# A new order of steps in the first two token blocks, score banks turned round, and a wait taken out of the last expert

## The chip, the cores and the metric

The kernel is one program on one NeuronCore of a Trainium2 chip. The metric is the device time of one execution in microseconds (us), lower is better. The engines are named as in the profile: PE is TensorE (PEld its weight loads), DVE is VectorE, ACT is ScalarE, POOL is GpSimd, SP is SyncE, which here only issues DMAs.

## What is computed

An input x of 4 x 1024 tokens with 256 features goes through gated cross-attention and a gated mixture of experts:

```python
x = x + tanh(g_xattn) * attention(layernorm(x), ctx, ctx)   # 16 heads of 16, 77 context rows per batch
h = layernorm(x)                                            # with gain and bias
logits = h @ Wr                                             # 7 experts, top 2 chosen, softmax gates
routed = experts(h)       # capacity 732 tokens: silu(h @ W1[e]) * (h @ W3[e]) @ W2[e], times the gate
shared = silu(h @ W1s) * (h @ W3s) @ W2s                    # every token
x = x + tanh(g_ffn) * (routed + shared)
```

All is fp32. Each large product is made of three passes with operands split in a high and a low part (hi*hi, hi*lo, lo*hi), so most tiles exist twice: a cast gives the high part, a subtraction the low one.

## The kernel before, in words

**Blocks.** The 4096 tokens are 8 blocks of 512 (four tiles of 128). Attention of block b and the shared network of block b-1 are interleaved by hand in one list of steps for each period: `first_period` (block 0), `second_period` (block 1), `period` (blocks 2 to 6, in a loop of two and one more) and `last_period` (block 7). Each engine walks through the same list and takes out of it the steps that it has code for, so the list sets every engine's own order, and each engine runs strictly in that order, stopping at semaphores. After the blocks come the seven experts (`expert`), each with weights that have been loaded and split while the one before ran.

**Attention of a block.** PE transposes normalized x (`transpose_x`), makes the queries (`queries`), and computes per tile of 128 tokens scores against all keys only for their maxima (`maxima`; DVE reduces them, and the next tile's matmuls use the same banks and wait for that reduction). `maxima_T` transposes the 16 x 512 maxima, ACT copies them out (`mtr`), SP stacks them by DMA under the queries in `qst` (`stack_maxima`), where keys `kst` carry a row of -1 for each head, so that one matmul of 112 rows gives scores less their maximum (`pair_scores`, a pair of heads p from 0 to 7). Pairs 0 and 1 are scored in `first_scores`, the others in `scores`, each pair in two of the four banks 0 to 3, followed by an exponential of 77 x 1024 on ACT (`exps`) and the products with the values (`pv`, two pairs at a time). DVE transposes the result back and divides; ACT and POOL split it (`attention_hi`, `attention_lo`), and PE projects it (`project`). DVE adds it to x and takes statistics, POOL makes the reciprocal root, DVE normalizes (`norm2`), PE transposes again (`transpose_z`), ACT and DVE apply gain and bias and split.

**Shared network.** `up(f)` is 12 matmuls of 512 columns in two banks (`up_a`, `up_b`), ACT's silu, DVE's product, a cast and a subtraction; `down(f)` is 12 matmuls of 256 columns over four tiles. Banks 0 to 2 rotate for `up`.

**Shared weights in the first block.** Six half matrices h = 0 to 5 (W1s, W3s, W2s) are loaded into staging areas that are used again (h = 4 uses the area of h = 2). ACT casts each in two pieces (`shared_hi`), POOL subtracts (`shared_lo`, one piece of 512 columns each, pieces 2h and 2h+1). SP loads h = 3 in the step `more_shared` after `xT_ready`, and h = 4 and 5 only after POOL's piece 5:

```python
if h > 3:
    sp.wait_ge(sig["wsplit_lo"], NSTEP0 + 6)
```

POOL's code for the step `scores` is `attention_lo`; in block 0 it waits there until all attention of the block is done. `keep_busy(j, n, ...)` is n small matmuls into bank j that compute nothing needed.

**Last expert.** Experts add their rows to the output with indirect DMAs that accumulate (L1084). The last expert's second half of rows is instead gathered from the output first (L1068, `rows_of_last`), added on DVE (L1652) and written back without accumulation.

Of the kernel before, what the change touches and what calls it, by code (L numbers as in the profile page):

```python
# [86 lines left out]
def first_period(do, b):  # L87
# [45 lines left out]
    do("scores", b, 1)  # L133
    do("queries", n)
# [12 lines left out]
    do("maxima", n, 2)  # L147


def second_period(do, b):  # L150
# [55 lines left out]
    up(6)  # L206
    nxt("maxima", 2)
    down(4)
    nxt("maxima", 3)
    do("pick", b, 1)  # L210
    down(5)
# [3 lines left out]
    nxt("exp_table")  # L215
    down(6)
    do("last_hidden", f)
    nxt("first_scores")
# [6 lines left out]
def period(do, b):  # L225
# [71 lines left out]
    down(5)  # L297
    nxt("maxima_T")
    nxt("stack_maxima")
    up(7)  # L300
    nxt("exp_table")
    if not odd:
        do("place", f, 0)
    down(6)
    do("last_hidden", f)
    nxt("first_scores")
# [166 lines left out]

def queries_bank(b):

    return 6 if b.at(1) else 4
# [33 lines left out]
def xT_bank(b):  # L510

    return 4 if b.at(1) else 6
# [31 lines left out]
def build(nc, a, out):  # L544
# [37 lines left out]
    mtr = ar(138, N)[0:H]  # L582

# [107 lines left out]
    qst0_loaded qst0_rest_loaded qst_loaded qst_rest_loaded kst_loaded kbd_spread heads_ready kbd_loaded vst_ready m_ready m_done mT_ready mtr_ready  # L691
# [35 lines left out]
    def q_of(b):  # L727

        return hTs[0] if b.at(0) else qT

# [8 lines left out]
    def _(sp):  # L739
# [29 lines left out]
        def first_keys():  # L769

            sp.wait_ge(sig["k_lo"], KD)
            for j in range(2):
                sp.dma_start(kscr[j].rearrange("(k p) t -> p k t", p=P), k_s[:, j].bitcast(F32)).then_inc(sig["k_stored"], 16)
# [5 lines left out]
        def load_keys(b):  # L779

            if b.c == 0:
# [9 lines left out]
                sp.wait_ge(sig["k_stored"], 32)  # L791
# [27 lines left out]
        def stack_rest(b):  # L819

            for r in (2, 3):
                for base in (0, 64):
                    sp.dma_start(qst[base:base + 32, r::4, :].bitcast(F32), q_of(b)[32 * r:32 * r + 32, 0].bitcast(F32)).then_inc(sig["qst0_rest_loaded"], 16)

        def stack_maxima(b):
            sp.wait_ge(sig["mtr_ready"], b.n + 1)

            first, rest = ("qst0_loaded", "qst0_rest_loaded") if b.at(0) else ("qst_loaded", "qst_rest_loaded")
            for r0, r1, loaded in ((0, 2, sig[first]), (2, NPAIR, sig[rest])):
                sp.dma_start(qst[96:112, r0:r1, :].bitcast(F32),  # L830
                             mtr[:, :].bitcast(F32).unsqueeze(1).broadcast_to([H, r1 - r0, N])).then_inc(loaded, 16)
                if b.at(0) and r0 == 0:
                    stack_first_lo((2, 3), sig[rest])
# [42 lines left out]
    def _(pool):  # L876
# [33 lines left out]
        def rest_const():  # L910
# [3 lines left out]
                                  pattern=[[1, P]], channel_multiplier=-1))  # L914
            do(pool.memset(vst[0:SK], 1.0))
# [147 lines left out]
        def rows_of_last(e):  # L1063
# [7 lines left out]
            pool.wait_ge(sig["rows_gathered"], 16 * (NR // 2))  # L1071
# [23 lines left out]
    def _(act):  # L1095
# [35 lines left out]
        def stack_hi(b):  # L1131
# [3 lines left out]
            for r in range(2):  # L1135
                for base in (0, 64):
                    act.dma_start(qst[base:base + 32, r::4, :].bitcast(F32), q_of(b)[32 * r:32 * r + 32, 0].bitcast(F32)).then_inc(sig["qst0_loaded"], 16)
# [5 lines left out]
        def transpose_x(b):  # L1143
            for k in range(KD):
# [9 lines left out]
        def maxima_T(b):  # L1154
            act.wait_ge(sig["mT_ready"], b.n + 1)
            if b.at(1):
                act.wait_ge(sig["qst0_loaded"], 112)
# [3 lines left out]
        def exps(b, p):  # L1161
# [5 lines left out]
            act.activation(prob[p % 4][0:SK], banks[0:SK, 2 * (p % 2):2 * (p % 2) + 2], ACT.Exp, scale=DH ** -0.5)\  # L1167
               .then_inc(sig["exp_done"], 1)

        def first_scores(b):  # L1170
            for p in range(2):
                exps(b, p)
# [970 lines left out]
```

## Time and profile before

| | us |
|---|---|
| median of three executions | 852.79 |
| lowest, highest | 852.49, 857.55 |
| profiled execution | 850.94 |
| its span (first to last instruction) | 849.2 |
| its mean granted TensorE clock, share of full speed | 0.997 |

The span is what the views below divide; 1.74 us of the profiled execution lie around it. Time stamps are from the start of the span. In a timeline row the numbers are start and duration (of one instruction, or from the first to the last of a merged run), then engine, line, operation, tile and count, and in brackets the idle time of that engine just before and what ended it.

### The profile page before, as it was taken

The numbers are of one execution on the slowest core, as the hardware profiler recorded it, in microseconds if no ns is written. First come the engines' busy times: TensorE is split into PE (matmuls) and PEld (weight loads), VectorE is DVE, ScalarE is ACT, GpSimd is POOL, SyncE is SP. The second block draws the span as 40 slices with busy tenths as digits, with TensorE's granted clock in tenths as the row PEclk, the third lists the DMA queues.
The fourth block names the chain that finished last, engine by engine and source line by source line (L and its number), as shares of the span: only waits on it lengthen the run. The fifth ranks groups of instructions, "written<-read, shape, count | busy, mean of one in ns | idle before, by whom it ended". The sixth has DMA issues, their size and how long they took to land.

```text
span 849.2 us, 14564 instructions
## 1 busy us (share of the span) xinstructions
PE 821.0 (97%) x5228; PEld 719.8 (85%) x5228; DVE 588.6 (69%) x1260; ACT 386.2 (45%) x660; POOL 321.6 (38%) x250
## 2 busy tenths in 40 slices
PE   8888999999999999999999999999999999999995
PEld 7474868868868688687788899999999999999995
DVE  7577788787788777888877666565656756566442
ACT  4547263373453633734445454453544545354331
POOL 7453103150032230303126405818275481834336
PEclk9999999999999999999999999999999999999998
DMA  8541411324104223130032624334444324431112
GB/s 265 136 125 28 125 38 35 90 53 119 19 25 124 43 52 85 34 100 14 26 125 53 194 75 108 71 83 105 110 88 88 102 46 112 98 76 17 16 25 38
DMA packets 92257, 67.24 MB, mean 79 GB/s; under 512 B 53556, under 2 KB 78984, under 8 KB 92200
## 3 DMA queue, kind: packets, MB, share of 16 engines
q1 hardware_dynamic: 39608, 54.79, 23.1%
q0 software_dynamic: 51744, 10.67, 8.8%
q10 hardware_dynamic: 848, 1.05, 0.5%
q8 instruction: 31, 0.51, 0.3%
q14 instruction: 26, 0.21, 0.1%
HBM read 37.75 MB, written 14.27 MB: 61 GB/s over the span
## 4 chain that ended last, share of the span: by engine, by line
PE 81%; DVE 4%; issue 3%; ACT 1%; POOL 1%; DVEq 0%; POOLq 0%; ACTq 0%
PE bank L1692 20%; PE bank L1694 20%; PE bank L1693 20%; PE bank L1993 3%; PE bank L1994 3%; PE bank L1995 3%; PE bank L1832 2%; PE bank L1826 2%; PE bank L1793 2%; PE bank L2035 1%; PE bank L1931 1%; PE bank L2019 1%; PE bank L1699 1%; PE bank L1922 1%; PE bank L1700 1%
## 5 line engine op out<-in xcount | busy, mean ns | idle before, releaser
L1692 PE MATMUL bank<-split_operands 128*128 128x366 f32 (+4 forms) x1104 | 364.9, 331 | 1.6 <-POOL split_operands L972 0.9
L1694 PE MATMUL bank<-split_operands 128*128 128x366 f32 (+4 forms) x1104 | 359.6, 326 | 0.0
L1693 PE MATMUL bank<-split_operands 128*128 128x366 f32 (+4 forms) x1104 | 359.5, 326 | 0.0
L1692 PEld LDWEIGHTS bank<-split_operands 128*128 128x128 f32 (+1 forms) x1104 | 205.8, 186 | 17.7 <-issue 5.9
L1694 PEld LDWEIGHTS bank<-split_operands 128*128 128x128 f32 (+1 forms) x1104 | 205.5, 186 | 10.6
L1693 PEld LDWEIGHTS bank<-split_operands 128*128 128x128 f32 (+1 forms) x1104 | 206.0, 187 | 8.1
L1084 POOL DMA_INDIRECT out<-float_data,scatter_now x42 | 120.1, 2860 | 170.1 <-DVE float_data L1655 146.7
L1675 DVE TENSOR_TENSOR hidden<-bank,float_data 128x366 f32<-128x366 f32 x112 | 60.5, 540 | 108.3 <-PE bank L1694 108.0
L1270 ACT ACTIVATE float_data<-bank 128x366 f32<-128x366 f32 x112 | 53.5, 477 | 110.2 <-PE bank L1694 110.2
L1267 ACT CAST split_operands<-hidden 128x366 fp32r<-128x366 f32 x112 | 55.7, 497 | 68.5 <-DVE hidden L1675 68.5
L1046 POOL DMA_INDIRECT float_data<-z_scratch,gather_now x42 | 72.9, 1736 | 17.6 <-issue 16.1
L1669 DVE TENSOR_TENSOR split_operands<-hidden,split_operands 128x366 fp32r<-128x366 f32 x112 | 60.4, 539 | 18.6 <-ACT split_operands L1267 18.6
L1993 PE MATMUL bank<-split_operands 128*128 128x256 f32 x256 | 73.1, 286 | 0.0
L1994 PE MATMUL bank<-split_operands 128*128 128x256 f32 x256 | 72.4, 283 | 0.0
L1995 PE MATMUL bank<-split_operands 128*128 128x256 f32 x256 | 72.3, 283 | 0.0
L1221 ACT ACTIVATE float_data<-bank 128x512 f32<-128x512 f32 x64 | 38.3, 599 | 60.1 <-PE bank L1694 57.8
L1428 DVE TENSOR_TENSOR split_operands<-hidden,split_operands 128x512 fp32r<-128x512 f32 x64 | 49.3, 770 | 20.2 <-ACT split_operands L1202 20.1
L1438 DVE TENSOR_TENSOR hidden<-bank,float_data 128x512 f32<-128x512 f32 x64 | 43.8, 684 | 23.2 <-PE bank L1694 22.9
L1167 ACT ACTIVATE float_data<-bank 77x1024 f32<-77x1024 f32 x48 | 47.2, 1017 | 16.7 <-PE bank L1832 15.8
L1211 ACT CAST split_operands<-float_data 128x512 fp32r<-128x512 f32 x84 | 50.8, 612 | 5.4 <-DMA float_data<-in_L_ffn_W 5.4
L1202 ACT CAST split_operands<-hidden 128x512 fp32r<-128x512 f32 x64 | 39.5, 618 | 27.4 <-DVE hidden L1438 27.4
L1993 PEld LDWEIGHTS bank<-split_operands 128*128 128x128 f32 x256 | 48.7, 190 | 2.9 <-DVE split_operands L1428 1.3
(177 smaller groups left out, 1116.1 us busy)
## 6 DMA issues: line engine op xcount, KB each, us to landing
float_data<-in_L_ffn_W SPq DMA_DIRECT2D x21, 1024.0 KB, 7.8
split_operands<-split_operands SPq DMA_DIRECT2D x92, 128.0 KB, 2.4
float_data<-in_x SPq DMA_DIRECT2D x8, 512.0 KB, 4.4
z_scratch<-float_data SPq DMA_DIRECT2D x8, 512.0 KB, 3.1
out<-float_data SPq DMA_DIRECT2D x7, 512.0 KB, 2.9
split_operands<-split_operands SPq DMA_DIRECT2D x8, 192.0 KB, 3.8
float_data<-in_L_ffn_W1s SPq DMA_DIRECT2D x2, 512.0 KB, 9.4
float_data<-in_L_ffn_W3s SPq DMA_DIRECT2D x2, 512.0 KB, 7.6
```

The lines of the kernel that those rows point to most:

```text
L1046: pool.indirect_dma_start(xg[e.c][0:RT, t, :], None, zscr, bass.IndirectOffsetOnAxis(ap=gidx[e.c][0:RT, t:t + 1].bitcast(U32), axis=0))\
L1084: pool.indirect_dma_start(out2, bass.IndirectOffsetOnAxis(ap=sidx[e.c][0:RT, t:t + 1].bitcast(U32), axis=0), ye[0:RT, t, :], None, bounds_ ...
L1267: act.copy(hidden_at(e, n - 1)[:, 0], gf[:, (n - 1) % 2, 0:HALF]).then_inc(sig["gh_ready"], 1)
L1270: act.activation(sil[n % 2][:, 0:HALF], bank[2 * (n % 2)][:, 0:HALF], ACT.Silu)\
L1669: dve.tensor_tensor(g[:, 1], gf[:, (n - 1) % 2, 0:HALF], g[:, 0].bitcast(F32), ALU.subtract)\
L1675: dve.tensor_tensor(gf[:, n % 2, 0:HALF], bank[2 * (n % 2) + 1][:, 0:HALF], sil[n % 2][:, 0:HALF], ALU.mult).then_inc(sig["gmul_done"], 1)
L1692: pe.matmul(o, lhs[0], rhs[0], start=first, stop=False)
L1693: pe.matmul(o, lhs[0], rhs[1], start=False, stop=False)
L1694: return pe.matmul(o, lhs[1], rhs[0], start=False, stop=last)
L1993: pe.matmul(o, lhs[0], rhs[0], start=(f == 0 and t % 2 == 0), stop=False, skip_group_check=True)
L1994: pe.matmul(o, lhs[0], rhs[1], start=False, stop=False, skip_group_check=True)
L1995: mm = pe.matmul(o, lhs[1], rhs[0], start=False, stop=(f == NF - 1), skip_group_check=True)
```

## The change

1. **Block 0 scores.** Pairs 0 and 1 no longer take their maxima out of `qst`. Their score is a matmul of 96 rows and a second one that accumulates `neg` (16 rows of 0 and -1, made by POOL in `rest_const`) times `mtr` directly. `first_scores` then waits for the copy `mtr` instead of a DMA. ACT issues all eight stacking DMAs of the high queries, SP keeps the low ones, and the first 77 columns of the keys are stored to DRAM first with a semaphore of their own.
2. **Block 0 order.** `shared_hi(2, 3)` and `shared_lo(4, 6)` move behind the scores of block 0; `more_shared` moves with the shorter `shared_lo(0, 4)`. `values_out` goes ahead of `scale_x`. Block 1's transposed x goes to banks 6 and 7 and behind `first_scores`, and DVE makes its high part instead of ACT. One filler step of 3 replaces two of 8 and 4.
3. **Block 0 `transpose_z`.** ACT computes the full-precision value (`full`), DVE only subtracts (`low_z`), after `maxima(n, 2)`. Block 1's goes to ACT too.
4. **Block 1.** Six filler matmuls become two. `scale_x` of block 2 goes between the halves of the scores, `transpose_x` of block 2 ahead of `up(3)`, a silu table load ahead of that, and `project_second` does high products before it waits for low parts.
5. **All blocks from 2 on.** Even pairs take banks 2 and 3, odd ones 0 and 1; `up` banks rotate by one. PE scores pair 0 right behind `up(7)`, pair 1 behind `down(6)` (`second_scores`); ACT's exponentials stay behind `last_hidden`. `up(6)` is cut in halves with a tile of `down` and `maxima(2)` between, and `maxima_T` comes after the first tile of `down(5)`.
6. **Last expert.** POOL no longer waits for its three gathers before it goes on to the scatters of the first half.

```diff
@@ first_period
     do("stack_maxima", b)
-    do("shared_hi", 2, 3)
+    do("values_out")
     do("scale_x", n)
-    do("shared_lo", 0, 1)
-    do("values_out")
-    do("shared_lo", 1, 6)
+    do("shared_lo", 0, 4)
+    do("more_shared")
+    do("keep_busy", 2, 3, "m_done", TT)
+    do("first_scores", b)
     do("transpose_x", n)
-    do("more_shared")
-    do("keep_busy", 2, 8, "m_done", TT)
-    do("first_scores", b)
-    do("keep_busy", 6, 4, "v_ready", B)
     do("route_const")
     do("scores", b, 0)
     do("scores", b, 1)
+    do("shared_hi", 2, 3)
+    do("shared_lo", 4, 6)
     do("queries", n)
...
     do("transpose_z", b)
     do("maxima", n, 2)
+    do("low_z", b)
@@ second_period
-    do("keep_busy", 6, 6, "hl_ready", KD)
+    do("keep_busy", 6, 2, "hl_ready", KD)
     nxt("stats_x")
-    nxt("scale_x")
     do("hidden", f, 2)
     nxt("keys")
     do("scores", b, 0)
+    nxt("scale_x")
     do("scores", b, 1)
+    do("silu_table")
+    nxt("transpose_x")
     up(3)
     do("attention_hi", b)
-    nxt("transpose_x")
     do("project", b)
...
-    up(6)
+    do("up_a", f, 6)
+    down(4, 0, 1)
     nxt("maxima", 2)
-    down(4)
+    do("up_b", f, 6)
+    down(4, 1, 2)
     nxt("maxima", 3)
     do("pick", b, 1)
+    down(4, 2, TT)
@@ period
     nxt("maxima", 1)
-    up(6)
+    do("up_a", f, 6)
+    down(3, 2, 3)
     nxt("maxima", 2)
-    down(3, 2, TT)
-    down(4, 0, 3)
+    do("up_b", f, 6)
+    down(3, 3, TT)
     nxt("maxima", 3)
-    down(4, 3, TT)
+    down(4)
...
-    down(5)
+    down(5, 0, 1)
     nxt("maxima_T")
     nxt("stack_maxima")
+    down(5, 1, TT)
     up(7)
     nxt("exp_table")
+    nxt("first_scores")
     if not odd:
         do("place", f, 0)
     down(6)
     do("last_hidden", f)
-    nxt("first_scores")
+    nxt("second_scores")
@@ helpers
+def score_banks(p):
+    return slice(2, 4) if p % 2 == 0 else slice(0, 2)
+def up_bank(f, w):
+    return (2 * f + w + 1) % 3
@@ rows_of_last (POOL)
-            pool.wait_ge(sig["rows_gathered"], 16 * (NR // 2))
@@ transpose_z (ACT), low_z (DVE)
+            if b.at(0):
+                for k in range(KD):
+                    full(b, k)
...
+        def low_z(b):
             for k in range(KD):
...
-                dve.tensor_tensor(hTs[b.c][:, 1, k], hf[:, :], hTs[b.c][:, 0, k].bitcast(F32), ALU.subtract)\
+                dve.tensor_tensor(hTs[b.c][:, 1, k], full_of(b, k), hTs[b.c][:, 0, k].bitcast(F32), ALU.subtract)\
@@ pair_scores (PE)
+                if b.at(0) and p < 2:
+                    pe.matmul(banks[0:SK, score_banks(p).start + w, :], kst[0:96, p, w, :], qst[0:96, p, :], start=True, stop=False)
+                    mm = pe.matmul(banks[0:SK, score_banks(p).start + w, :], neg[:, p, w, :], mtr[:, :], start=False, stop=True)
+                    continue
@@ first_scores (PE)
-                pe.wait_ge(sig["gmul_done"], (b.n - 1) * NF)
-            for p in range(2):
-                pair_scores(b, p)
+                pe.wait_ge(sig["gmul_done"], (b.n - 2) * NF + 7)
+            pair_scores(b, 0)
+            if b.at(0) or b.at(1):
+                pair_scores(b, 1)
@@ first_scores (ACT)
+            if b.at(0) or b.at(1):
+                second_scores(b)
@@ project_second (PE, new, block 1)
+            pe.wait_ge(sig["ah_ready"], (b.n + 1) * KD)
+            high(0)
+            pe.wait_ge(sig["xl_ready"], (b.n + 2) * KD)
+            for t in (1, 2):
+                high(t)
+            pe.wait_ge(sig["al_ready"], (b.n + 1) * KD)
+            for t in range(3):
+                low(t)
+            pe.wait_ge(sig["x1_ready"], b.n * TT + 1)
+            high(3)
+            low(3)
```

## Rows read from the trace of the kernel before

**Rows 1.** The page: span, and its first part, busy time per engine.

```profile
span 849.2 us, 14564 instructions
PE 821.0 (97%) x5228; PEld 719.8 (85%) x5228; DVE 588.6 (69%) x1260; ACT 386.2 (45%) x660; POOL 321.6 (38%) x250
```

**Rows 2.** The waits of PE, whole span: total, times, longest.

```profile
PE bank L1826 <- ACT probabilities L1167: 4.4, 8, 0.6
```

**Rows 3.** The timeline of PE, block 0, second half of the scores.

```profile
31.81 1.16 PE L1832 MATMUL bank<-split_operands 112*77 112x512 f32 x4 [1.48 <-DMA split_operands<-split_operands]
```

**Rows 4.** The timeline of ACT, then of SP's queue, block 0.

```profile
23.65 0.57 ACT L1159 CAST split_operands<-bank 16x512 fp32r<-16x512 f32 x1 [2.64 <-PE bank L1800]
...
19.06 4.30 SPq L796 DMA_DIRECT2D split_operands<-k_scratch  x6
...
27.90 0.60 SPq L830 DMA_DIRECT2D split_operands<-split_operands  x1
...
32.21 0.94 SPq L763 DMA_DIRECT2D float_data<-in_L_ffn_W2s  x2
```

**Rows 5.** DMA issues of 32.0 to 32.5 us: size, median us to landing.

```profile
float_data<-in_L_ffn_W2s SPq DMA_DIRECT2D x1, 512.0 KB, 3.4
```

**Rows 6.** The timeline of POOL behind block 0's attention.

```profile
42.35 2.52 POOL L972 TENSOR_TENSOR split_operands<-float_data,split_operands 128x512 fp32r<-128x512 f32 x2 [9.02 <-DVE float_data L1381]
44.84 5.00 POOL L961 TENSOR_TENSOR split_operands<-float_data,split_operands 128x512 fp32r<-128x512 f32 x4
50.17 0.19 POOL L991 TENSOR_SCALAR var_scaled<-mean_var 128x4 f32<-128x4 f32 x1 [0.33 <-issue]
```

**Rows 7.** The timeline of PE, then of DVE, around block 0's `transpose_z`.

```profile
47.54 3.51 PE L1732 MATMUL bank<-ident 128*128 128x128 f32 x30
...
52.12 1.59 PE L1922 MATMUL bank<-ident,float_data 128*128 128x128 f32 x8
...
55.08 2.01 PE L1950 MATMUL bank<-split_operands 128*128 128x512 f32 x8
57.37 1.21 PE L1954 MATMUL bank<-split_operands 128*128 128x512 f32 x4 [0.28 <-DVE split_operands L1414]
58.79 0.87 PE L1793 MATMUL bank<-split_operands 128*128 128x462 f32 x4 [0.20 <-DVE row_max L1355]
...
55.05 0.69 DVE L1414 TENSOR_TENSOR split_operands<-normed_heads,split_operands 128x512 fp32r<-128x512 f32 x1
...
57.23 1.11 DVE L1353 TENSOR_REDUCE row_max<-bank 128x12 f32<-128x924 f32 x1
```

**Rows 8.** The timeline of PE, then of DVE, block 1.

```profile
82.08 1.09 PE L1746 MATMUL bank<-ident,float_data 128*128 128x128 f32 x8 [1.81 <-DVE float_data L1381]
84.09 0.39 PE L1692 MATMUL bank<-split_operands 128*128 128x256 f32 x1 [0.91 <-POOL split_operands L972]
...
71.85 1.38 DVE L1332 TENSOR_SCALAR float_data<-float_data,mean_var,rstd 128x256 f32<-128x256 f32 x4 [1.62 <-POOL rstd L924]
```

**Rows 9.** The timeline of the later blocks: ACT, DVE and PE.

```profile
120.21 1.02 ACT L1167 ACTIVATE float_data<-bank 77x1024 f32<-77x1024 f32 x1 [0.49 <-PE bank L1832]
...
160.76 1.11 DVE L1353 TENSOR_REDUCE row_max<-bank 128x12 f32<-128x924 f32 x1
...
165.33 0.89 PE L1793 MATMUL bank<-split_operands 128*128 128x462 f32 x4 [0.22 <-DVE row_max L1355]
```

**Rows 10.** The timeline of POOL, then of DVE, at the end.

```profile
820.27 1.67 POOL L1068 DMA_INDIRECT float_data<-out,gather_now  x1 [0.30 <-issue]
827.25 2.97 POOL L1084 DMA_INDIRECT out<-float_data,scatter_now  x1 [5.32 <-issue]
...
841.34 1.66 POOL L1084 DMA_INDIRECT out<-float_data,scatter_now  x1 [0.30 <-issue]
...
839.31 0.48 DVE L1652 SCALAR_TENSOR_TENSOR float_data<-bank,gates_now,float_data 122x256 f32<-122x256 f32 x1 [2.34 <-PE bank L1694]
```

**Rows 11.** Busy us of PE, PEld, DVE, ACT, POOL; granted clock, DMA share, GB/s.

```profile
844.00:845.00 1.00, 0.00 (x0) 0.00 (x0) 0.00 (x0) 0.00 (x0) 0.00 (x0) 0.50 0.45 64
```

More of the change, by code:

```diff
@@ L296, in period @@
         do("pick", b, 1)
-    down(5)
+    down(5, 0, 1)
     nxt("maxima_T")
     nxt("stack_maxima")
+    down(5, 1, TT)
     up(7)
     nxt("exp_table")
+    nxt("first_scores")
     if not odd:
@@ L305, in period @@
     do("last_hidden", f)
-    nxt("first_scores")
+    nxt("second_scores")
     if not odd:
@@ L729, in q_of, with full_of @@
         return hTs[0] if b.at(0) else qT
+    def full_of(b, k):
+        return gf[:, 1] if b.at(0) and k == 1 else hf[:, :]
     def apart(eng):
@@ L819, in stack_rest @@
         def stack_rest(b):
-            for r in (2, 3):
-                for base in (0, 64):
-                    sp.dma_start(qst[base:base + 32, r::4, :].bitcast(F32), q_of(b)[32 * r:32 * r + 32, 0].bitcast(F32)).then_inc(sig["qst0_rest_loaded"], 16)
+            stack_first_lo((2, 3), sig["qst0_rest_loaded"])
         def stack_maxima(b):
             sp.wait_ge(sig["mtr_ready"], b.n + 1)
[L828 to L833, printed above, removed]
+            for r0, r1, loaded in ((0, 2, sig["qst_loaded"]), (2, NPAIR, sig["qst0_rest_loaded" if b.at(0) else "qst_rest_loaded"])):
+                if not b.at(0) or r0 > 0:
+                    sp.dma_start(qst[96:112, r0:r1, :].bitcast(F32),
+                                 mtr[:, :].bitcast(F32).unsqueeze(1).broadcast_to([H, r1 - r0, N])).then_inc(loaded, 16)
         def store_z(b):
@@ L1335, in transpose_x @@
         def transpose_x(b):
+            if b.at(1):
+                for k in range(KD):
+                    dve.wait_ge(sig["xT_ready"], KD + k + 1)
+                    dve.tensor_copy(xT[:, 0, k], bank[xT_bank(b) + k][:, :]).then_inc(sig["xh_ready"], 1)
             for k in range(KD):
@@ L1831, in pair_scores @@
             for w in range(2):
-                mm = pe.matmul(bank[2 * (p % 2) + w][0:SK, :], kst[0:112, p, w, :], qst[0:112, p, :], start=True, stop=True)
+                if b.at(0) and p < 2:
+                    pe.matmul(banks[0:SK, score_banks(p).start + w, :], kst[0:96, p, w, :], qst[0:96, p, :], start=True, stop=False)
+                    mm = pe.matmul(banks[0:SK, score_banks(p).start + w, :], neg[:, p, w, :], mtr[:, :], start=False, stop=True)
+                    continue
+                mm = pe.matmul(banks[0:SK, score_banks(p).start + w, :], kst[0:112, p, w, :], qst[0:112, p, :], start=True, stop=True)
             mm.then_inc(sig["scores_ready"], 1)
@@ L1889, in project_first, with project_second, high, low @@
                     mm.then_inc(sig["oproj_ready"], 1)
+        def project_second(b):
+            aT, w = q_of(b), [wat[:, j, 3] for j in range(2)]
+            out = [bank[project_bank(b, t)][:, 0:D] for t in range(TT)]
+            at = [slice(t * P, (t + 1) * P) for t in range(TT)]
+            def high(t):
+                for k in range(KD):
+                    for j in range(2):
+                        pe.matmul(out[t], aT[:, 0, k, at[t]], w[j][:, k], start=(k + j == 0), stop=False)
+            def low(t):
+                for k in range(KD):
+                    mm = pe.matmul(out[t], aT[:, 1, k, at[t]], w[0][:, k], start=False, stop=(k == KD - 1))
+                mm.then_inc(sig["oproj_ready"], 1)
+            pe.wait_ge(sig["ah_ready"], (b.n + 1) * KD)
[9 more added lines that the diff above has]
+            low(3)
         def project(b):
@@ L1893, in project @@
                 project_first(b)
+                return
+            if b.at(1):
+                project_second(b)
                 return
@@ L1949, in first_up @@
                     for j in range(2):
-                        pe.matmul(bank[w][:, :], W0[:, j, w, k * FF:k * FF + P], hTs[0][:, 0, k], start=(k + j == 0), stop=False)
+                        pe.matmul(bank[up_bank(0, w)][:, :], W0[:, j, w, k * FF:k * FF + P], hTs[0][:, 0, k], start=(k + j == 0), stop=False)
             pe.wait_ge(sig["hl_ready"], KD)
@@ L1953, in first_up @@
                 for k in range(KD):
-                    mm = pe.matmul(bank[w][:, :], W0[:, 0, w, k * FF:k * FF + P], hTs[0][:, 1, k], start=False, stop=(k == KD - 1))
+                    mm = pe.matmul(bank[up_bank(0, w)][:, :], W0[:, 0, w, k * FF:k * FF + P], hTs[0][:, 1, k], start=False, stop=(k == KD - 1))
                 mm.then_inc(ready, 1)
```

73 lines of the change are left out of this document (52 added, 21 removed).

## The prediction

> **What bounds the kernel now.** I read the page first: PE is busy for 821.0 of 849.2 us [rows 1], so all that any order of steps can win is 28.2 us of PE idle time, plus filler matmuls that stand in for idle time. Next the waits of PE, whole span: the largest is that of `pv` for the exponentials, 4.4 us in eight waits, one per block, up to 0.6 each [rows 2]. Then the timeline of each stretch that the change touches, PE's first (when does it stop, for whom), then the engine it waits for, and what that engine did before. Five stretches come out: the start of block 0's scores, where PE waits for a stacking DMA [rows 3]; block 0's `transpose_z` [rows 7]; block 1's end of attention [rows 8]; the repeating end of a period [rows 9]; and the last scatters [rows 10]. Everything between is PE back to back, so a gain or loss in one stretch goes through to the end, and the sum is made of the five.
>
> **1. Start of block 0's scores: 3.2 us earlier, at first.** PE starts the second half of the scores at 31.81 when the last stacking DMA lands [rows 3]. That DMA was issued at 27.90 [rows 4], so it took 3.9. In the changed kernel `first_scores` waits for the ACT copy of the maxima (ends 24.22 [rows 4]; ACT now issues four more DMAs before it, so perhaps 0.2 later) and for the keys. Their six DMAs began at 19.06 and took 4.30 to issue [rows 4]; with the shorter store ahead I take the start 0.7 earlier and about 2.5 for the last to land, so 25.1. Pairs 0 and 1 then cost four matmuls more, 0.25 each (eight of 512 columns in 2.01 [rows 7]), and the eight transposes of block 1 (1.1 to 1.6, as in [rows 7, 8]) go behind them. The DMA of the other pairs needs only the copy and the two low stacks: issued at 24.5, plus 3.9, lands at 28.4. So the second half starts at about 28.6 instead of 31.81: 3.2 gained. From there to the end of attention the chain ACT, PE, DVE is the same; DVE's four split operations of block 1's x (0.69 each [rows 7], 2.7) fit in its idle time. If the ACT queue is late, the gain is 2.5.
>
> **2. Between attention and `transpose_z`: the 3.2 is lost, and 0.9 more.** Here the order of POOL and SP decides. POOL stands in `attention_lo` until block 0's attention is over: it started at 42.35 after 9.02 of idle time [rows 6]. The change puts pieces 4 and 5 of the shared weights behind that point, where before POOL did them ahead of that idle time. The load of half matrix 4 waits for piece 5. It was issued at 32.21 [rows 4], long ahead of any use; now: POOL starts at 42.35 - 3.2 = 39.15, two splits of attention 2.5, two pieces at 1.25 (four in 5.00 [rows 6]) 2.5, so piece 5 is done at 44.15 and the load is issued at 44.2. It lands 3.4 later [rows 5], 47.6; ACT casts (0.6), POOL subtracts pieces 8 and 9 from 48.3 to 50.8. Behind them in POOL's order stands `norm2`, the reciprocal root for block 0, which ran at 50.17 [rows 6] and would now have been wanted at 47.0. With 0.2 to 0.3 between instructions it runs at 51.05. So `transpose_z` starts at 52.12 + 0.9 = 53.0 [rows 7], though attention ended 3.2 earlier. SP also stands in that wait, and behind it block 1's stacking of queries, which is not wanted before block 1's scores. PE has no work there: filler and `maxima(n, 1)` end 3.2 earlier, at about 49.1 (filler 47.54 plus 3.51, minus 3.2, then one group of 0.87 [rows 7]), so it idles 3.9.
>
> If that wait cost nothing, this stretch would keep the 3.2; if the load took 5, it would lose 1.6 more than I take. The value is the nearest row, the same load.
>
> The granted clock bears on this gap. After PE's last matmul, which precedes the DVE instruction at 839.31 [rows 10], the clock in 844 to 845 reads 0.50, the lower of the two levels, 1.2 instead of 2.4 GHz [rows 11]: idle for some 4.7 us, it had fallen. The gap that I expect is shorter, so I take no fall; it is a rival. The Trainium skill, "TensorE: Matmul & The Clock Gate", section "What's actually happening", says that the throttled state is the default and that activity releases it; by that, the fall in the last rows is the ordinary result of idleness, and taking out filler is not free. The trace agrees for its end, and shows nothing for a gap of 3.9.
>
> **3. `transpose_z` itself: 0.55 slower.** ACT takes two operations from DVE, but DVE now reduces `maxima(n, 2)` before it subtracts. Before: transposes at 52.12, low parts of `up(0)` at 57.37, the third maxima at 58.79, `up(1)` 0.7 later [rows 7]: 7.4 from the first transposes. After, counted from the same point: the reduction of maxima 1 ends at 2.1, PE's maxima 2 ends at 3.1, its reduction (1.11 and 0.47, 57.23 to 58.79 with the wait [rows 7]) at 4.75, two subtractions (0.69 each) at 6.1, then four matmuls (1.1), maxima 3 (0.75): `up(1)` at 7.95. Bounds 0 and 1. Together with 2, `up(1)` starts 1.45 later than before.
>
> **4. Block 1: 2.3 gained.** DVE waited 1.62 for POOL and then took 1.38 for `scale_x` [rows 8] with the first transposes behind it; PE later stood 1.81 and 0.91 [rows 8]. Now `scale_x` lies between the halves, `transpose_x` in front of `up(3)`, which covers DVE's remaining chain, and `project_second` begins before POOL's part. Going through DVE's order, attention ends 1 to 1.8 earlier, and the wait of 1.81 is covered by `up(3)`. The two waits, 2.7, are the upper end, with 0.4 for shorter filler 3.1; the lower is 1.4 (scale_x off the path alone). A residue remains, for the ACT copy, now behind the silu table load, and the high products' wait: 2.3.
>
> **5. End of each period: 2.3 lost.** One sees the aim in [rows 2] and [rows 9]: exponentials start earlier. But they follow `last_hidden` on ACT, and pair 1 and the third pair stay behind `down(6)` and `down(7)` in PE's order. After the first two, ACT already waited 0.49 for PE's third pair [rows 9]. Exponentials 0 and 1 earlier by 0.55 make this wait longer and change nothing behind it. So the 0.5 before the last `pv` stays, six times.
> The cut of `up(6)` moves maxima 2 1.0 nearer to maxima 1. In even periods DVE has one-hot tables to make first, so it starts the reduction of maxima 1 at 160.76 [rows 9] and is done at 162.3. PE reaches maxima 2 at 161.65: it came to maxima 3 at 165.11 (165.33 less 0.22 [rows 9]); back from there five tiles at 0.36, maxima 2 at 0.75 and `up` at 2.75 give 159.8 for the start of `up(6)`, plus 1.4 for its half and 0.36 for a tile. It waits 0.65, later 0.25 for the reduction before `maxima_T`, and the old 0.22 goes: 0.65 each, say 0.6, in three periods. In the two odd periods no tables lie ahead; up to 0.3 before `maxima_T`, taken as 0.15. That is 2.1. In block 1's period the maxima's DMA lands about 0.35 after `up(7)`, and some 0.2 of old waits go: 0.2. The lower end is a gain of 0.7 (old 0.22 waits gone, none new), the upper a loss of 4.
>
> **6. Tail: 1.5 gained.** POOL's last gather issue ends at 821.94; the first scatter started at 827.25 after 5.32 of waiting [rows 10]. Without it, three scatters at about 3.2 each end at 832, long before the last three. The last one started at 841.34 because it queued behind them, though its data were ready at 839.79 [rows 10]: it can start at 840.3, 1.0 earlier. DMA traffic of accumulating scatters no longer overlaps it, so it may land sooner by up to 1.5. I take 1.5 in all; 1.0 to 2.5.
>
> **Sum.** +0.9 +0.55 -2.3 +2.1 +0.2 -1.5 = about 0. The profiled execution took 850.94, so 850.9 after; the median of the runs shown is 1.85 higher, 852.79, and I carry that: **852.7**. The terms' own bounds leave 849 to 857.
>
> **Rivals.**
> A. *The weight load does not hold POOL, or the exponentials do gain.* For it: [rows 2] is the largest wait, and ACT is busy 45% only [rows 1]. Then part 2 keeps its 3.2 (4.1 better than my sum), or the six waits of 0.5 go (3.0 better), or the maxima do not wait (2.8). Two of them: 846; all: 843. Against: the order of the queues. Chance 0.22.
> B. *The cut `up(6)` hurts more, slower than before.* DVE is 69% busy [rows 1] and the maxima share one set of banks; if DVE reaches the reduction of maxima 1 0.6 later than in the row shown in every period, five periods lose 0.6 more each, and POOL's traffic on shared tables the same again in the even ones: 857. It decides as soon as the reduction ends more than 1.75 after maxima 1's matmuls. Chance 0.15.
> C. *The clock falls in block 0's gap.* Then the 16 transposes and matmuls behind it (about 3.4 us of PE work) run at half speed: part of it is covered by DVE, 1 to 3 more: 855. It decides from a gap near the tail's 4.7. The same page's rule speaks for it. Chance 0.1.
> My forecast: 0.53, itself 849.5 to 856.
>
> **Numbers.** The range: A's upper half and B and C inside, 846 to 857. A measurement of this kernel can tell about 1% (8.5 us) from no change. Faster than 844.3 needs nearly all of A: 0.09. Slower than 861.3 needs B and C at once: 0.04. Within 1%: 0.87.
>
> **What would show it.** In the changed profile: scores' second half near 28.6; the load of h = 4 issued near 44.2 and POOL's root near 51, with a PE gap of about 4 us before block 0's `transpose_z`; waits for the exponentials still near 0.5 in each block; new waits of maxima 2 for row_max of about 0.6 in even periods; no wait of POOL before the scatter at 822. I am wrong if that gap is missing, or if the exponentials' wait has gone.

## The result, and the profile after

The changed kernel is slower: 860.05 us (median of 16 executions, 857.86 to 864.85) against 852.67 for the kernel before (16 executions). The ratio is 1.0083, 95% interval 1.0063 to 1.0103, so 5 to 9 us were lost. The profiled execution took 863.93, its span 862.2; it is one of the longer ones, as the profiled one of the kernel before (span 849.2) is one of the shorter, so the traces lie 13.0 apart and the medians 7.4. The mean granted clock, recorded for every execution, sorts the sixteen: six with 0.976 to 0.980 took 862.89 to 864.85, the profiled one among them, and ten with 0.987 to 0.991 took 857.86 to 861.14. What the trace shows below is therefore the worse of two cases. The prediction, 852.7 within 846 to 857, was wrong.

The page of the changed kernel, its first two parts (40 slices of the span, 21.6 us each):

```profile
span 862.2 us, 14523 instructions
PE 833.0 (97%) x5206; PEld 723.6 (84%) x5206; DVE 585.9 (68%) x1258; ACT 388.7 (45%) x663; POOL 322.9 (37%) x252
...
PE   8889999999999999999999999999999999999995
...
PEclk9678999999999999999999999999999999999998
```

PE is busy 97% of the span, as in [rows 1], but it is busy 12 us longer with 22 matmuls fewer. The same work took longer, and the clock row says where: 6, 7 and 8 in the second to fourth slice. Most of the difference is made in the first 65 us: block 0's `transpose_z` starts at 63.96 instead of 52.12 [rows 7], 11.8 of the 13.0 later.

The waits of PE, 20 to 122 us:

```profile
PE bank L1892 <- DMA split_operands<-k_scratch: 3.3, 1, 3.3
PE bank L2024 <- DVE float_data L1457: 2.9, 1, 2.9
```

Two long waits are new. To see what they are, the timeline of PE in block 0, which answers to [rows 3] and [rows 7]:

```profile
24.11 0.83 PE L1790 MATMUL bank<-ident 128*128 128x128 f32 x6
28.23 0.52 PE L1892 MATMUL bank<-split_operands 96*77 96x512 f32 x1 [3.29 <-DMA split_operands<-k_scratch]
...
34.75 2.06 PE L1895 MATMUL bank<-split_operands 112*77 112x512 f32 x4
...
60.13 0.88 PE L1853 MATMUL bank<-split_operands 128*128 128x462 f32 x4 [0.37 <-DVE row_max L1408]
63.96 2.21 PE L2024 MATMUL bank<-ident,float_data 128*128 128x128 f32 x8 [2.95 <-DVE float_data L1457]
```

`maxima_T` and what is left of the filler (the row at 24.11) end at 24.94. The first scores start at 28.23, not at 25.1: they wait for the keys. And the four matmuls of 112 rows take 2.06 where they took 1.16 in [rows 3]. Next, busy time and clock in stretches of 4 us (busy PE, PEld, DVE, ACT, POOL; clock; DMA share; GB/s):

```profile
24.00:28.00 4.00, 0.94 (x9) 0.75 (x6) 2.22 (x7) 1.39 (x3) 3.00 (x3) 1.00 0.97 169
28.00:32.00 4.00, 3.77 (x7) 1.30 (x7) 0.00 (x0) 1.02 (x1) 4.00 (x8) 0.55 0.17 23
32.00:36.00 4.00, 4.00 (x13) 2.77 (x14) 1.56 (x3) 1.03 (x2) 0.55 (x5) 0.50 0.00 0
...
48.00:52.00 4.00, 4.00 (x10) 3.17 (x11) 2.54 (x5) 1.28 (x2) 1.69 (x2) 0.50 0.00 0
52.00:56.00 4.00, 4.00 (x31) 3.81 (x30) 2.10 (x5) 1.72 (x3) 4.00 (x4) 0.96 0.01 4
...
60.00:64.00 4.00, 0.92 (x5) 0.68 (x5) 0.68 (x3) 1.14 (x2) 3.19 (x4) 0.82 1.08 265
64.00:68.00 4.00, 3.92 (x14) 3.01 (x15) 2.42 (x6) 2.58 (x4) 0.00 (x0) 0.50 1.00 262
```

A reader who looks at "busy" alone sees a full PE from 28 on. It is full at 1.2 GHz (0.50), and PE, not ACT, now sets the pace. ACT waits for it before nearly every exponential:

```profile
33.24 1.02 ACT L1196 ACTIVATE float_data<-bank 77x1024 f32<-77x1024 f32 x1 [1.46 <-PE bank L1893]
35.99 1.02 ACT L1196 ACTIVATE float_data<-bank 77x1024 f32<-77x1024 f32 x1 [1.73 <-PE bank L1895]
```

The clock fell to 0.50 at the end of a gap of 3.3 us and stayed there for some 24 us, until block 1's dense `queries` had run a while. It fell again after the gap before `transpose_z`. The chain that fills the second gap, ACT's, POOL's and SP's timelines (they answer to [rows 4] and [rows 6]):

```profile
16.66 6.03 ACTq L1163 DMA_DIRECT2D split_operands<-split_operands  x8
...
19.10 5.36 SPq L823 DMA_DIRECT2D split_operands<-k_scratch  x6
...
55.38 0.94 SPq L786 DMA_DIRECT2D float_data<-in_L_ffn_W2s  x2
...
50.31 2.53 POOL L999 TENSOR_TENSOR split_operands<-float_data,split_operands 128x512 fp32r<-128x512 f32 x2 [17.76 <-DVE float_data L1434]
52.80 5.04 POOL L988 TENSOR_TENSOR split_operands<-float_data,split_operands 128x512 fp32r<-128x512 f32 x4
59.47 2.50 POOL L988 TENSOR_TENSOR split_operands<-float_data,split_operands 128x512 fp32r<-128x512 f32 x2 [1.63 <-ACT split_operands L1154]
62.05 0.19 POOL L1018 TENSOR_SCALAR var_scaled<-mean_var 128x4 f32<-128x4 f32 x1
```

From POOL's start at 50.31, the load of h = 4 is issued 5.07 later and the root runs 11.74 later. Part 2 of the prediction had 5.05 and 11.9.

### The profile page after: what moved, and what is told of

It is laid out like the page before. It is cut to its first block, busy times and chain, and to the rows that moved or that the text cites. A ratio compares the mean times of both kernels' runs of the same rounds, so it can differ in the third digit from the quotient of the medians.

```text
span 862.2 us, 14523 instructions
## 1 busy us (share of the span) xinstructions
PE 833.0 (97%) x5206; PEld 723.6 (84%) x5206; DVE 585.9 (68%) x1258; ACT 388.7 (45%) x663; POOL 322.9 (37%) x252
## 4 chain that ended last, share of the span: by engine, by line
PE 85%; DVE 4%; issue 3%; DMA 3%; POOL 2%; ACT 1%; SPq 1%; DVEq 0%; ACTq 0%; POOLq 0%
PE bank L1750 20%; PE bank L1752 19%; PE bank L1751 19%; PE bank L1895 4%; PE bank L1885 3%; PE bank L2095 3%; PE bank L2096 3%; PE bank L2097 3%; PE bank L1853 2%; DMA float_data<-in_L_ffn_W 1%; PE bank L2137 1%; PE bank L2033 1%; PE bank L1806 1%; DVE row_max L1406 1%; PE bank L2121 1%
## 5 line engine op out<-in xcount | busy, mean ns | idle before, releaser
L2095 PEld LDWEIGHTS bank<-split_operands 128*128 128x128 f32 x256 | 48.7, 190 | 3.4 <-DVE split_operands L1486 1.0
```

The costliest lines, as they stand in the source:

```text
L2095: pe.matmul(o, lhs[0], rhs[0], start=(f == 0 and t % 2 == 0), stop=False, skip_group_check=True)
```

## The experiments

Each was compared with runs of the kernel before on the same chip; there were three such groups of experiments, each on a chip of its own. The kernel before has executions of its own in which the clock falls in block 0 (see the last section), so its medians differ a little between the groups (852.67 to 853.81), and where a tenth matters I compare traces. The changed kernel itself was timed only once, as reported above.

**Filler back ahead of the scores.**

```diff
-    do("keep_busy", 2, 3, "m_done", TT)
+    do("keep_busy", 2, 17, "m_done", TT)
```

> The changed kernel with 17 filler steps instead of 3 ahead of first_scores, so that PE is busy until the keys land at 28.2; nothing else moves. Theory C (the granted clock that falls in the 3.3 us gap costs most of the time): clock 1.00 from 28 to 52, scores to attention's end 7 to 9 us shorter, 851 to 854 in all (the later gap before transpose_z may still bring the clock down for some 6 us). Rival W (the waits themselves cost the time, the clock little): filler changes nothing, 858 to 861.

Measured 856.13, ratio 1.0029 (1.0001 to 1.0057); profiled span 853.3: 8.9 shorter than the changed kernel by the traces, 3.9 by the medians. The traces overstate it, since one is of the slower six of the changed kernel and the other is the fastest of twelve. Its PE timeline, and the stretch of 28 to 32 by the columns above:

```profile
24.08 3.96 PE L1790 MATMUL bank<-ident 128*128 128x128 f32 x34
27.80 0.47 PE L1892 MATMUL bank<-split_operands 96*77 96x512 f32 x1
28.20 0.45 PE L1893 MATMUL bank<-split_operands 16*77 16x512 f32 x1
28.57 0.45 PE L1892 MATMUL bank<-split_operands 96*77 96x512 f32 x1
```
```profile
28.00:32.00 4.00, 4.00 (x18) 2.07 (x17) 0.43 (x1) 2.04 (x2) 4.00 (x8) 1.00 0.22 27
```

Filler fills PE from 24.08 until the keys are there, and it starts the scores at nearly the same point as without (27.80 against 28.23), so the real work began only 0.43 earlier, and yet `maxima(n, 0)` came at 46.89 instead of 55.65. That is theory C; rival W falls. Ten of the twelve executions have a mean clock of 0.992 or more (855.04 to 857.91); the other two, at 0.980 and 0.978, took 862.17 and 862.69, so filler makes the long fall rare and does not rule it out. The version stays above the kernel before by the second gap (3.65 us, clock 0.58 in 56 to 60) and the periods' ends.

**The converse, on the kernel before: filler out.**

```diff
-    do("keep_busy", 2, 8, "m_done", TT)
     do("first_scores", b)
-    do("keep_busy", 6, 4, "v_ready", B)
```

> The kernel before with its two filler steps around first_scores (8 and 4) taken out; no wait of the real work changes, PE stands idle for about 3.3 us and then 2.5 us instead of twice 1.5. Theory C: the clock falls in this stretch in all or some executions and stays down until the dense queries, 5 to 9 us longer, 858 to 862. Rival W: filler has no effect on the time, 852.7 within 1.

Measured 859.25, ratio 1.0055 (1.0032 to 1.0078). The PE timeline:

```profile
28.33 1.88 PE L1830 MATMUL bank<-split_operands 112*77 112x512 f32 x4 [3.29 <-DMA split_operands<-split_operands]
31.73 1.99 PE L1830 MATMUL bank<-split_operands 112*77 112x512 f32 x4 [1.52 <-DMA split_operands<-split_operands]
```

The scores start at 28.33 and 31.73, as with filler (28.29 before, 31.81 [rows 3]), but the four matmuls take 1.88 and 1.99 instead of 1.15 and 1.16. Here the clock fell every time: all twelve executions have a mean clock of 0.980 to 0.984. Taking 24 matmuls that compute nothing out of the kernel before costs 5.6 us by the medians, most of what the change loses.

**Filler, and the shared weights in their old order.**

```diff
     do("stack_maxima", b)
+    do("shared_hi", 2, 3)
...
-    do("shared_lo", 0, 4)
+    do("shared_lo", 0, 6)
...
     do("scores", b, 1)
-    do("shared_hi", 2, 3)
-    do("shared_lo", 4, 6)
```

> As the run with 17 filler steps, and the two casts and two subtractions of the shared weights (h = 2, pieces 4 and 5) back in their old place ahead of the scores, so that SP loads h = 4 early. If POOL's order costs what part 2 of the prediction says: POOL's root runs about 4 us earlier against the end of attention, no PE gap before transpose_z and no second fall of the clock, 848 to 850; that is 3 to 5 below the run with filler alone. Rival (the gap is covered by something else then late): within 1 us of it.

Measured 851.68, ratio 0.997 (0.9942 to 0.9999), 4.45 below the one with filler alone. `transpose_z` starts at 52.68 instead of 55.88, 0.7 is the largest wait between 43 us and it, and the clock is 1.00 from 24 to 68 us. POOL's and SP's order delays `transpose_z` by 3.2 and brings a fall of the clock behind it, 4.45 in all; part 2 had 4.1 without a fall. One execution of the twelve (859.37, mean clock 0.984) still fell.

**Which DMA makes the keys late.** ACT issues four of the high stacks (`stack_hi`, the first pair of lines), SP the other four behind the keys (`stack_rest`, ahead of the low parts), the rest as in the changed kernel.

```diff
-            for r in range(4):
+            for r in range(2):
...
+            for r in (2, 3):
+                for base in (0, 64):
+                    sp.dma_start(qst[base:base + 32, r::4, :]...)
```

> The changed kernel with four of the eight stacking DMAs of the high queries back on SP, behind the keys' DMAs, as before the change; filler stays 3. Theory A (the four more DMAs on ACT's queue make the keys' DMAs late): the keys land by about 25.5 instead of 28.2, the first gap shrinks below 1 us. Rival S (the keys' store in two parts with rows of 308 bytes does it): keys land near 28 as they do now. In both the last stacking DMA comes near 31, so a second gap of 2 to 3 us may replace the first: 852 if the clock stays up, 858 to 861 if it falls.

Measured 860.25, ratio 1.0049 (1.0023 to 1.0075). The PE timeline:

```profile
25.86 0.43 PE L1895 MATMUL bank<-split_operands 96*77 96x512 f32 x1 [0.91 <-DMA split_operands<-k_scratch]
...
31.57 1.99 PE L1898 MATMUL bank<-split_operands 112*77 112x512 f32 x4 [1.06 <-DMA split_operands<-split_operands]
```

The keys land 2.4 us earlier: the four more DMAs of 128 KB, issued by ACT just ahead of the keys', made them late, and the store in two parts did not. The keys' DMAs take 2.0 to 3.6 us to land here and 4.2 to 5.1 in the changed kernel. That ACT's queue as such matters, and not only four more DMAs in flight, is not shown: the edit moves them in time too. The last stack then comes at 31.57, where it was before the change (31.81). And the clock fell here too (four matmuls of 112 rows in 1.99), though the two waits are only about 1 us each: it is 0.83 in 28 to 30, ahead of the second wait, and 0.50 from 30 to 48. The shorter waits gained nothing.

**Ten filler steps.** The filler line with 10 in place of 3.

> The changed kernel with 10 filler steps instead of 3, so that the first gap is about 1.5 us, like those of the kernel before, instead of 3.3. Theory C in its simple form (a gap of 1.5 us is harmless, one of 3.3 is not): as with 17 steps, 855 to 856.5. Rival (the clock looks at how much PE does around the gap, and the scores are thin): it falls here too in part of the executions, 858 to 860.

Measured 857.35, ratio 1.0056 (1.0032 to 1.008). The wait is 1.48 us, and behind it the clock fell for some 4 us (0.84 in 30 to 32, 0.50 in 32 to 34, 0.80 in 34 to 36), against 24 in the traced execution of the changed kernel. So neither theory is quite right: the clock fell behind a gap of 1.5 us, but came back soon. That the length of the gap decides how long the fall lasts is not shown: with four stacks on ACT a wait of 0.91 was followed by one of 20 us.

**The ends of the periods as before**, on top of filler and old weight order: `up(6)` whole, tiles of `down` and `maxima_T` where they were, and

```diff
     nxt("exp_table")
-    nxt("first_scores")
...
     do("last_hidden", f)
+    nxt("first_scores")
     nxt("second_scores")
```

> The version with 17 filler steps and the old order of the shared weights, and in addition the end of every period as before the change: up(6) whole, the tiles of down where they were, maxima_T behind down(5), pairs 0 and 1 scored together behind down(6); only the turned banks stay. By part 5 of the prediction and by the traces (2.07 us lost between the transpose_z of blocks 1 and 7) it is about 2 us faster than the version it is made from, 849.5 to 850, with one wait of 0.2 for the row maxima per even period again instead of 0.65. Rival (the turned banks cost the time, not the order): no gain, 851.5 to 852.

Measured 849.98, ratio 0.9952 (0.9932 to 0.9972), 1.7 below the version with the change's period ends. From block 1's `transpose_z` to block 7's it took 329.7 us against 332.0 with the change's order and 330.0 in the kernel before. The turned banks, still there, cost nothing. Block 0 is that of the version with filler and the old weight order. There the clock stayed at 1.00 behind a wait of 0.40; here it fell for some 4 us in the traced execution, behind a wait of 0.37 (four matmuls of 112 rows in 2.05).

```profile
28.35 0.43 PE L1886 MATMUL bank<-split_operands 96*77 96x512 f32 x1 [0.37 <-DMA split_operands<-k_scratch]
32.74 2.05 PE L1889 MATMUL bank<-split_operands 112*77 112x512 f32 x4
```

**The cut of `up(6)` undone, with the tiles of `down` and `maxima_T` that had moved for it**, pair 0 still early.

> As the run before this one, but pair 0 stays behind up(7), ahead of down(6). If the cut of up(6) makes all of the loss, it is as fast as that one (849.5 to 850). If the early pair costs something by itself (two matmuls more that stand alone among matmuls of another kind, or the wait for the maxima's DMA), it is 0.5 to 1 slower. If the early pair gains what the change was made for, the waits for the exponentials (0.5 each) shrink and it is 1 to 3 faster; I expect no shrinking.

Measured 852.76, ratio 0.9994 (0.9967 to 1.0021), and 332.2 us between the same points. The cut by itself does not make the loss. Without it and with `maxima_T` back behind `down(5)`, PE waits for the maxima's DMA before pair 0:

```profile
230.06 0.68 PE L1889 MATMUL bank<-split_operands 112*77 112x512 f32 x2 [0.42 <-DMA split_operands<-split_operands]
```

There are six such waits of 0.20 to 0.43, 1.9 us together, of the 2.5 that this version loses to the one before it. So without the early `maxima_T` pair 0 comes too early for its maxima, and with it and the cut there are other waits, one per even period, as in the changed kernel's timeline of PE (it answers to the wait of 0.22 in [rows 9]):

```profile
173.45 0.87 PE L1853 MATMUL bank<-split_operands 128*128 128x462 f32 x4 [0.65 <-DVE row_max L1408]
```

Behind block 0 the waits for the exponentials stayed at 0.48 to 0.57 in every version.

**Four of ACT's stacks later** (`stack_late`: those of rows 2 and 3, taken out of `stack_hi`), on top of the version with the old period ends, 12 filler steps.

```diff
     do("shared_hi", 0, 2)
+    do("stack_late", b)
-    do("keep_busy", 2, 17, "m_done", TT)
+    do("keep_busy", 2, 12, "m_done", TT)
```

> The first of this call with four of ACT's eight stacking DMAs issued only after its first four casts of the shared weights, and 12 filler steps instead of 17. Theory A (these four make the keys late): keys land by 26.5 to 27, PE starts the scores there and their second half near 30 instead of 32.3; 1.5 to 2 us faster than the first, 848. Rival (the four are late themselves now): the second half waits until 31 to 32, no gain, and if PE stands idle long enough the clock falls, 855 and more.

Measured 851.83, ratio 0.9977 (0.9954 to 1.0). A miss: ACT's queue issued them at 19.3 to 22.5, beside the casts and not behind them, the keys landed at 28.08 as before, PE waited 1.31 and the clock fell for some 6 us. With 1.9 us more than the version it was made from (849.98), it is no gain.

**Filler in the middle.** Four steps in bank 4 just ahead of the second half of block 0's scores.

```diff
     do("first_scores", b)
     do("transpose_x", n)
+    do("keep_busy", 4, 4, "m_done", TT)
```

> The version with the old period ends and 17 filler steps (its median 849.98), with four filler steps more behind block 1's transposes, just ahead of the second half of block 0's scores, into bank 4. There the clock fell for some 3 us at 32 in the profiled execution, behind first_scores alone. If thin scores need filler in the middle (theory C with activity, not only gaps): clock 1.00 throughout block 0, first half of a us to 1 us gained in executions that fell, 0.9 lost to the filler: 849.5 to 850.5 with a narrower spread. Rival (the fall has to do with the gap alone, 0.37 at 28): the clock still falls, 851.

Measured 850.55, ratio 0.9955 (0.9937 to 0.9973): no gain. In the profiled execution the clock was 0.92 in 28 to 32 and 0.65 in 32 to 36, so it fell before the new filler (at 33.73) could act, behind a wait of 0.60 and in the eight matmuls of `first_scores`.

**The tail alone**, on the kernel before.

```diff
-            pool.wait_ge(sig["rows_gathered"], 16 * (NR // 2))
```

> The kernel before with POOL's wait for its three gathers in the last expert taken out, nothing else. By part 6 of the prediction 1 to 2.5 us from the end of PE's last matmul to the end of the span (9.9 us before); by the changed kernel's trace 0.6 (9.3 us). No difference that the time of the runs can tell.

Measured 850.58, ratio 0.9966 (0.9938 to 0.9995). From the start of the last DVE addition to the end of the span it takes 848.8 - 839.46 = 9.34, before 849.2 - 839.31 = 9.89 [rows 10]: 0.55 gained by the trace, more than that by the ratio, whose interval reaches to 0.4. The medians lie 3.2 apart mostly because the clock fell more seldom: one of these ten executions has a mean clock of 0.992 or less, and 16 of the 29 of the kernel before. As block 0 is the same code, I count that as chance. The executions at 0.997 took 849.83 to 850.55, against 850.55 to 850.91.

**Block 1 and the tail alone**, on the kernel before: `second_period` down to `project_second` as in the change, block 2's transposed x in banks 4 and 5, the tail as above.

> The kernel before with the change's block 1 (scale_x between the halves, transpose_x of block 2 ahead of up(3) in banks 4 and 5, the silu table load, project_second, two filler steps instead of six) and its tail, but block 0 and the ends of the periods as before. By part 4 and the traces 1.7 us from block 1 and 0.6 from the tail: 850 to 850.5, 2.3 below the kernel before, clock 0.997. Rival (block 1's gain is owed to block 0's new order, or shorter filler lets the clock fall here): no gain, or more than 853.

Measured 848.96, ratio 0.9948 (0.9921 to 0.9976). The profiled execution (span 851.1) is one of five of the twelve in which the mean clock is 0.989 or less (852.79 to 855.89; the other seven took 848.20 to 849.05). The clock fell in block 0, whose code here is that of the kernel before:

```profile
28.00:32.00 4.00, 2.37 (x14) 1.79 (x15) 0.00 (x0) 1.93 (x2) 4.00 (x4) 1.00 0.92 191
32.00:36.00 4.00, 4.00 (x20) 1.42 (x22) 1.39 (x3) 2.97 (x4) 1.38 (x9) 0.71 0.74 261
```

**The same with six stacks on ACT and two on SP.** (The first pair of lines is `stack_hi`, the second `stack_rest`.)

```diff
-            for r in range(2):
+            for r in range(3):
...
-            for r in (2, 3):
+            for r in (3,):
```

> As the one before, and two of SP's four stacking DMAs of the high queries go to ACT (six there, two on SP). The keys' DMAs get later (25.9 with four on ACT, 28.2 with eight) to about 27, the maxima's DMA and the last one 1.2 earlier than at 28.3 and 31.8: the scores start near 27 and their second half at 30.6, 1.2 us faster than the one before, 849. Rival (each DMA on ACT delays the keys by 0.6 or more beyond that): the keys become the last arrival, no gain; with the fillers kept the clock holds either way.

Measured 847.56, ratio 0.9917 (0.9888 to 0.9946), all six executions within 847.13 to 848.01. It beats the kernel before by 6.25 us by the medians, and part of that is the clock: all six have a mean clock of 0.996 or 0.997. The PE timeline:

```profile
27.68 1.14 PE L1839 MATMUL bank<-split_operands 112*77 112x512 f32 x4 [0.77 <-DMA split_operands<-split_operands]
...
31.14 1.15 PE L1839 MATMUL bank<-split_operands 112*77 112x512 f32 x4 [1.43 <-DMA split_operands<-split_operands]
```

The two starts came 0.6 and 0.7 us earlier than before, half of what I expected. The first wait shrank from 1.44 to 0.77. Against the seven executions without a fall of the version it was made from, the gain is about 1.0 (median 847.56 against 848.53); that it also keeps the clock up is not shown, as six executions are few where five of twelve fell.

## Why the prediction was wrong

**Part 1 failed, and with it the reading of the clock.** The term was -3.2: "the keys ... about 2.5 for the last to land, so 25.1". They landed at 28.2. All three pieces of the term came out short. The keys' DMAs did not begin 0.7 earlier but at 19.10, as before: ahead of them on SP stood two stacking DMAs (17.44 to 18.97), which the shorter store does not move. They took 5.36 to issue instead of 4.30, and the last then landed some 3.8 later instead of 2.5. I priced the four more DMAs on ACT at 0.2 us of delay for ACT's own copy, and took the keys' landing from a trace in which those four did not run beside them. With four on ACT the keys land at 25.9. The copy `mtr` was mis-sized as well, 1.2 later instead of 0.2, behind 6.03 us of issuing and four casts:

```profile
22.73 2.18 ACT L1154 CAST split_operands<-float_data 128x512 fp32r<-128x512 f32 x4 [5.92 <-issue]
24.82 0.57 ACT L1188 CAST split_operands<-bank 16x512 fp32r<-16x512 f32 x1
```

It ended at 25.4, not at 24.4. The next term in the same part was short as well: I took 0.25 us for each of the matmuls of 96 and 16 rows, they follow each other in 0.38. So at full clock part 1 is worth nothing: the second half of the scores started at 31.73 with filler, 31.81 before. With four of the stacks left on SP the keys are nearly on time, but then the last stack comes at 31.57.

The miss of 3 us in an arrival would have cost only the 3.2, about 856 in all. The rest is the clock, which my sum put at nothing. I noted that filler stands in for idle time, and then looked for a fall only in the gap before `transpose_z`, at a chance of 0.1 and a price of 1 to 3. The first gap was not on my list, because in my sum it had no idle time: the filler that was to cover 25.1 ended at 24.9. Rival C had the mechanism, not the place and not the price. From the first gap its price was 8.9 us by the profiled executions and 3.9 by the medians, where I had 1 to 3: in the traced execution PE ran at half speed through all of the scores and the products with the values, with no idle time left to absorb it.

**Part 2 held.** POOL's root 11.74 after the start of `attention_lo` (11.9 predicted), PE's gap 2.95 in the changed kernel and 3.65 with filler (3.9 predicted, though the numbers I gave for its start add up to 48.7 and not 49.1, which makes it 4.3). I took no fall there; it fell in both. The order and that fall together are worth 4.45 us by the medians.

**Part 3 was right in sign only.** At full clock `transpose_z` to `up(1)` took 7.54 (52.68 to 60.22), 0.17 more than before; I had 0.55. This was measured with the shared weights in their old order; the term is small either way.

**Part 4 held in the mechanism, 1.7 instead of 2.3.** From `up(1)` to block 1's `transpose_z` 35.08 with filler and the old weight order, 36.74 before. Waits of 0.46 (x not normalized yet), 0.62 and 0.20 are left.

**Part 5 held.** 2.07 us lost from block 1's `transpose_z` to block 7's, 2.3 predicted; waits of 0.65, 0.62 and 0.63 in the even periods where I had 0.65; exponentials unchanged. The wait of 0.25 ahead of `maxima_T` that I had in the sum does not appear, and still the even periods lost 0.60, 0.63 and 0.59, so some 0.2 of each is in no wait. The cause was also less simple than I had it: the cut and the early pair depend on each other, and undoing the cut alone gains nothing.

**Part 6 was mis-sized, 0.6 instead of 1.5.** The term failed because the last scatter still queues behind two others of 2.0 each: the first of the three starts at 850.61 in the changed kernel although its data were ready at 849.57 and POOL free since 845.3. What held it for that 1.0 us is not shown. Before the change it stood 1.33 behind its data (835.98 to 837.31), so 0.3 of the 0.55 is here. POOL's timeline at the end, then DVE's, which answer to [rows 10]:

```profile
842.42 2.91 POOL L1110 DMA_INDIRECT out<-float_data,scatter_now  x1 [0.30 <-issue]
850.61 1.72 POOL L1110 DMA_INDIRECT out<-float_data,scatter_now  x1 [5.28 <-DVE float_data L1710]
...
854.63 1.67 POOL L1110 DMA_INDIRECT out<-float_data,scatter_now  x1 [0.30 <-issue]
...
849.09 0.48 DVE L1710 SCALAR_TENSOR_TENSOR float_data<-bank,gates_now,float_data 122x256 f32<-122x256 f32 x1 [1.27 <-PE bank L1752]
```

## What to carry to other kernels

Filler matmuls are part of the timing. Before taking one out, ask what arrives last behind it and by how much your estimate of that arrival may be off, because an error in an arrival turns into idle time, and idle time can turn into a clock that is half as fast for much longer than the gap (3.3 us of waiting, 24 of half speed in the traced execution). Read the mean granted clock of every execution beside its time: here it tells a slower kernel from an unlucky one. Price a DMA that is issued earlier, or on another queue, at what it does to every DMA in flight beside it, not at its issue time. And when a step waits for a whole group behind it (POOL in `attention_lo`), whatever is moved behind it takes along the loads that its result releases.

## What the runs showed of the hardware

The Trainium skill, "TensorE: Matmul & The Clock Gate", section "What's actually happening", has activity release the throttle. These traces agree that taking filler out brings the clock down: all twelve executions of the kernel before without filler have a mean clock of 0.980 to 0.984. But the length of the wait does not tell what follows. After 3.3 us the clock was low for about 24 us, after 1.48 for about 4, after 0.91 for about 20 (four stacks on ACT). With 17 filler steps and the same block 0 it stayed up behind a wait of 0.40 in one trace and fell behind 0.37 in another, in the eight matmuls of `first_scores`. Whether their new form, 96 and 16 rows in turn, has to do with it is not shown; no run puts the old form back into the changed kernel.

Nor does PE's busy time tell when the clock comes back. In the changed kernel PE has no idle time from 32 to 52 us, and the clock stays at 0.50. It rose at 52, with `queries` since 47.88; with four stacks on ACT it rose between 48 and 52, with `queries` since 44.64. With 10 filler steps it rose between 34 and 36, among the second half of the scores, where the changed kernel ran the same matmuls and stayed low. What makes that difference is open.

A kernel can sit on the edge of this. With the code of the kernel before in block 0, one profiled execution kept 1.00 and another fell to 0.71 and 0.50 at 32 to 48, and reached `transpose_z` 4 us later. It shows in the times without a trace: of 95 executions of the kernel before on three chips, the 12 with a mean clock of 0.997 took 850.55 to 851.48, and the 25 with 0.988 or less took 856.62 to 860.99.

Two matmuls of 512 columns that alternate between 96 and 16 rows follow each other in 0.38 us at full clock, those of 112 rows in about 0.25 (eight in 3.08 from 27.80 to 30.88, and four in 1.15). I had not expected the cost of splitting one matmul by rows in two to be threefold.
